# A recurrent attention and expert-gate kernel: the second output tile moves to bank_b, the experts' second product becomes two rounded passes

## What is computed

```python
xn = _layernorm(x, axis=-1)
# attention
q = (xn @ wq.T); k = (xn @ wk.T); v = (xn @ wv.T)        # 32, 8, 8 heads of 128
q = q * cos + _rotate_half(q) * sin; k = k * cos + _rotate_half(k) * sin
scores = einsum('bhqd,bhkd->bhqk', q, repeat(k)) / sqrt(128)  # scaled by key range, causal
attn = einsum('bhqk,bhkd->bhqd', softmax(scores), repeat(v))
s = attn.reshape(b, 256, 4096) @ wo.T
# experts
gates = softmax(top2(xn @ router_w.T))
mid = einsum('tf,erf->ter', xn, A)
all_deltas = einsum('ter,eor->teo', mid, B) * 4.0
g = silu(einsum('te,teo->to', gates, all_deltas))
return x + s * g
```

## Time and profile before

| | |
|---|---|
| median of 3 runs | 1377.58 us (1376.59 to 1377.71) |
| the profiled execution | 1377.09 us |
| its span, first to last instruction | 1375.3 us |
| mean granted TensorE clock | 0.991 |
| busy: PE, PE weight loads, DVE, ACT, POOL | 1335.1, 1105.3, 964.8, 962.2, 423.8 us |

### The profile page before, as it was taken

The page is one execution under the profiler, slowest core; times in us unless marked ns, Lnnn a source line. Parts: engine busy times, 40 slices in busy tenths (PEclk is TensorE's granted clock), DMA queues, the critical chain, the costliest instruction groups (busy, mean ns, idle before and its releaser), DMA issues.

```text
span 1375.3 us, 22613 instructions
## 1 busy us (share of the span) xinstructions
PE 1335.1 (97%) x6982; PEld 1105.3 (80%) x6982; DVE 964.8 (70%) x2444; ACT 962.2 (70%) x2512; POOL 423.8 (31%) x341
## 2 busy tenths in 40 slices
PE   7699999999999999999999999999999999999997
PEld 5588787777788888888888888888888888888885
DVE  6776577666766676776767677666777767668775
ACT  3687567667777767787777777777777767776773
POOL 5332221413414133143322234141331433224321
PEclk9799999999999999999999999999999999999998
DMA  5000000201101000000000001000000100012223
GB/s 210 16 16 14 23 16 9 69 24 31 69 1 31 0 23 23 0 31 15 23 8 15 15 15 31 0 31 0 23 23 0 31 15 23 8 43 87 69 81 104
DMA packets 23302, 43.48 MB, mean 32 GB/s; under 512 B 2464, under 2 KB 2592, under 8 KB 23264
## 3 DMA queue, kind: packets, MB, share of 16 engines
q1 hardware_dynamic: 20592, 37.76, 8.8%
q10 hardware_dynamic: 2672, 5.25, 1.0%
HBM read 34.61 MB, written 8.39 MB: 31 GB/s over the span
## 4 chain that ended last, share of the span: by engine, by line
PE 91%; DVE 5%; ACT 1%; issue 1%; DMA 1%; POOL 0%; DVEq 0%; SPq 0%; ACTq 0%
PE o_ps L542 26%; PE bank_a L447 18%; PE bank_b L447 18%; PE pv_ps L533 10%; PE pair L517 7%; PE pair L524 5%; PE pair L513 2%; DVE y_sum L1119 1%; PE o_ps L493 1%; PE pair L515 1%; PE bank_a L503 1%; PE o_ps L447 1%; DMA x_sb<-x 1%; DVE x_sb L946 0%; DVE xT_lo L959 0%
## 5 line engine op out<-in xcount | busy, mean ns | idle before, releaser
L362 POOL TENSOR_TENSOR rot<-rot,tab 128x512 f32<-128x512 f32 x160 | 208.6, 1306 | 611.5 <-ACT rot L749 611.3
L792 ACT ACTIVATE probs<-probs,row_min 128x128 f32<-128x128 f32 (+1 forms) x512 | 225.6, 447 | 0.0
L811 ACT ACTIVATE pT_hi<-pair 128x768 fp32r<-128x768 f32 x128 | 103.9, 812 | 170.2 <-PE pair L524 169.4
L542 PE MATMUL o_ps<-w_hi,attn_hi 128*128 128x512 f32 x504 | 206.8, 410 | 8.1 <-DVE y_sum L1119 7.0
L803 ACT ACTIVATE probs<-probs,row_inv 128x128 f32<-128x128 f32 (+1 forms) x512 | 190.8, 446 | 26.6 <-DVE row_inv L1109 26.3
L542 PE MATMUL o_ps<-w_hi,attn_lo 128*128 128x512 f32 x504 | 198.4, 394 | 0.0
L542 PE MATMUL o_ps<-w_lo,attn_hi 128*128 128x512 f32 x504 | 197.0, 391 | 0.0
L1079 DVE TENSOR_TENSOR pT_lo<-pair,pT_hi 128x768 fp32r<-128x768 f32 x128 | 121.5, 949 | 91.8 <-ACT pT_hi L811 91.6
L347 POOL TENSOR_TENSOR w_hi<-raw,zero 128x512 fp32r<-128x512 f32 x74 | 84.7, 1144 | 256.4 <-PE bank_a L447 135.6
L447 PE MATMUL bank_b<-xT_hi,w_hi 128*128 (+1 forms) x380 | 153.0, 403 | 2.4 <-DVE xT_lo L959 2.4
L447 PE MATMUL bank_a<-xT_hi,w_hi 128*128 (+1 forms) x380 | 154.6, 407 | 0.4 <-DVE xT_lo L959 0.4
(11 more groups left out here) (160 smaller groups left out, 2984.7 us busy)
## 6 DMA issues: line engine op xcount, KB each, us to landing
raw<-w_seq SPq DMA_DIRECT2D x76, 256.0 KB, 2.6
gate_scratch<-silu ACTq DMA_DIRECT2D x16, 256.0 KB, 2.0
out<-y_sum SPq DMA_DIRECT2D x16, 256.0 KB, 2.0
x_sb<-x SPq DMA_DIRECT2D x3, 1024.0 KB, 12.0
silu<-x SPq DMA_DIRECT2D x8, 256.0 KB, 2.7
silu<-gate_scratch SPq DMA_DIRECT2D x8, 256.0 KB, 2.8
bT_full<-x SPq DMA_DIRECT2D x7, 256.0 KB, 2.8
gmT_full<-gate_scratch SPq DMA_DIRECT2D x7, 256.0 KB, 3.0
```

Source lines behind the costliest of these rows:

```text
L362: nc.gpsimd.tensor_tensor(v, v, tab[:, s:s + SEQ].unsqueeze(1).to_broadcast([P, 2, SEQ]), ALU.mult).then_inc(sin_done[kind], 1)
L542: mm = nc.tensor.matmul(bank[:, :], a[:, h, rows], w[:, WO + h, :], start=(h == 0 and i == 0), stop=(h == GROUP - 1 and i == 2))
L792: a = nc.scalar.activation(s, s, ACT.Exp, bias=row_min[:, j % 2, i:i + 1], scale=-1.0, accum_out=row_sum[:, i:i + 1])
L811: nc.scalar.activation(pT_hi[:, :, :], pair[j % 2][:, :, 0:ROWS], ACT.Copy).then_inc(pThi_done, 1)
```

## The change

The second output tile of each pair, (0,1) and (1,1), is written to bank_b instead of o_ps, and DVE adds it from there. Tile (1,0) now waits for the addition of tile (0,0) (count 4u - 3) instead of tile (0,1); tile (1,1) and tile (0,1) wait that bank_b is free of H0 (in unit 30 of H3); the projection of H2 waits for the addition of tile (1,1). Side steps wait for one addition fewer. Tile (0,0) waits once for the last chunk of output weights. The last two tiles of all use pair0 instead of bank_a and bank_b.

The experts' second product becomes two fp32r passes: gm_T holds the rounded gate tile in partitions 0 to 63 and its remainder in 64 to 127, b_hi holds the rounded weights twice, b_lo the remainder once. The first pass has 128 contraction rows (both halves of gm_T with b_hi), the second 64 (rounded gate tile with b_lo). ACT rounds b in unit 1, DVE subtracts in unit 2; a gt step has ACT round and DVE subtract. The d steps go to slots 0 and 2 only, WRITTEN becomes 8, and the last d stands in slot (7,2,0). One buffer (b_raw) takes all gate tiles on their way out; it is stored in the slot behind its d. The sets xg take other buffers: mid, raw (loaded once the last weight chunks are split) and parts of rot and cosx (loaded behind the store of tile 11).

```diff
-WRITTEN = 7
+WRITTEN = 8
-        bT, gm_T = bT_full[0:ER, :], gmT_full[0:ER, :]
-        silu = sb("silu", [P, 2, DM])
+        b_raw = sb("b_raw", [P, DM])
+        b_hi = sb("b_hi", [P, DM], F32R)
+        b_lo_full = sb("b_lo", [P, DM], F32R)
+        b_lo = b_lo_full[0:ER, :]
+        gm_T = sb("gm_T", [P, BLOCK], F32R)
+        silu = b_raw
-        xg = [(silu[:, 0, :], silu[:, 1, :]), (bT_full[:, :], gmT_full[:, :]), (raw[:, 0, :], raw[:, 1, :])]
+        xg = [(mid_flat[:, 0:DM], mid_flat[:, DM:2 * DM]), (raw[:, 0, :], raw[:, 1, :]), (rot[:, 0, :], cosx[:, 0, :])]
-        places += [at for at in free if at >= (1, 2, 1) and at[2] != 3][:len(steps) - len(places)]
+        later = [at for at in free if at >= (1, 2, 1)]
+        for what, _ in steps[len(places):]:
+            while later[0][2] not in ((0, 2) if what == "d" else (0, 1, 2)):
+                later.pop(0)
+            places.append(later.pop(0))
...
-            load_xg(1, 1)
             for c in range(CHUNKS - 2, CHUNKS):
                 sp.wait_ge(w_ready[c], KV_HEADS)
-            load_xg(TILES - 1, 2)
+            load_xg(1, 1)
...
+            sp.wait_ge(q_ready[H2], UNITS)
+            load_xg(TILES - 1, 2)
             store_tile(TILES - 4)
...
-            tiles = 4 * u
+            tiles = max(0, 4 * u - 1)
...
-                nc.tensor.matmul(o_ps[:, :], gm_T[:, t * P:(t + 1) * P], bT, start=True, stop=True)\
+                nc.tensor.matmul(o_ps[:, :], gm_T[:, t * P:(t + 1) * P], b_hi[:, :], start=True, stop=False)
+                nc.tensor.matmul(o_ps[:, :], gm_T[0:ER, t * P:(t + 1) * P], b_lo, start=False, stop=True)\
                     .then_inc(side_ps, 1)
...
-            output_heads(b, t, o_ps, range(GROUP), weights=weights).then_inc(o_done, 1)
+            if weights is not None:
+                pe.wait_ge(w_ready[CHUNKS - 1], weights)
+            output_heads(b, t, (o_ps, bank_b)[t][:, :], range(GROUP)).then_inc(o_done, 1)
...
-                output_tile(1, 0, n4[0], n4[-2], uses=uses(0))
+                output_tile(1, 0, n4[0], n4[-3], uses=uses(0))
...
-                output_tile(1, 1, n4[0], n4[-1])
+                if not last:
+                    bank_free(H0, c2)
+                output_tile(1, 1, n4[0], n4[-2])
...
-                bank_free(H0, c2)
+                if first:
+                    bank_free(H0, c2)
+                else:
+                    pe.wait_ge(y_added, n4[0])
                 project(H2, bank_b, WQ + 2, x_1, w_1)
...
-            output_tile(0, 0, n4[2], None if first else n4[0], weights=w_0, uses=uses(3))
+            output_tile(0, 0, n4[2], None if first else n4[-1], weights=w_0, uses=uses(3))
...
-            output_tile(0, 1, n4[2], n4[1])
+            if not last:
+                bank_free(*((H0, c3) if ahead else (H3, c2)))
+            output_tile(0, 1, n4[2], n4[0] if last else None)
...
-                output_heads(1, t, (bank_a, bank_b)[t], range(0, 2))
+                output_heads(1, t, pair[0][:, t, :], range(0, 2))
...
-                nc.scalar.activation(gm_T, o_ps[0:ER, :], ACT.Copy).then_inc(side_out, 1)
+                nc.scalar.activation(gm_T[0:ER, :], o_ps[0:ER, :], ACT.Copy).then_inc(gmhi_done, 1)
...
+        def b_high():
+            nc.scalar.wait_ge(b_in, 32)
+            nc.scalar.activation(b_hi[:, :], b_raw[:, :], ACT.Copy).then_inc(bhi_done, 1)
...
-            nc.scalar.dma_start(bT, b_t).then_inc(bT_in, 16)
+            for half in range(2):
+                nc.scalar.dma_start(b_raw[ER * half:ER * (half + 1), :], b_t).then_inc(b_in, 16)
...
+        def split_b():
+            nc.vector.wait_ge(bhi_done, 1)
+            nc.vector.tensor_tensor(b_lo, b_raw[0:ER, :], b_hi[0:ER, :].bitcast(F32), ALU.subtract)\
+                .then_inc(blo_done, 1)
...
+            elif what == "gt":
+                dve.wait_ge(gmhi_done, i + 1)
+                nc.vector.tensor_tensor(gm_T[ER:, :], o_ps[0:ER, :], gm_T[0:ER, :].bitcast(F32), ALU.subtract)\
+                    .then_inc(side_out, 1)
```

More of the change, by code:

```diff
@@ L156, in build @@
         ar_in = sem("ar_in")
-        bT_in = sem("bT_in")
+        b_in = sem("b_in")
+        bhi_done = sem("bhi_done")
+        blo_done = sem("blo_done")
+        gmhi_done = sem("gmhi_done")
         stat_done = sem("stat_done")
@@ L263, in slots @@
         def slots(eng, u):
-            return {c: value(eng, 4 * u + c) for c in range(-2, 8)}
+            return {c: value(eng, 4 * u + c) for c in range(-3, 8)}
         def units(eng, u):
@@ L534, in prob_value, with output_heads @@
             mm.then_inc(pv_done, 1)
-        def output_heads(b, t, bank, heads, weights=None):
+        def output_heads(b, t, bank, heads):
             rows = slice(SEQ * b + P * t, SEQ * b + P * (t + 1))
             for h in heads:
-                if weights is not None:
-                    nc.tensor.wait_ge(w_ready[WO + h], weights)
                 for i, (a, w) in enumerate(((attn_hi, w_hi), (attn_hi, w_lo), (attn_lo, w_hi))):
-                    mm = nc.tensor.matmul(bank[:, :], a[:, h, rows], w[:, WO + h, :], start=(h == 0 and i == 0),
+                    mm = nc.tensor.matmul(bank, a[:, h, rows], w[:, WO + h, :], start=(h == 0 and i == 0),
                                           stop=(h == GROUP - 1 and i == 2))
@@ L699, in _ @@
             for t in range(2):
-                output_heads(1, t, (bank_a, bank_b)[t], range(0, 2))
+                output_heads(1, t, pair[0][:, t, :], range(0, 2))
             pe.wait_ge(attn_ready, n)
             for t in range(2):
-                output_heads(1, t, (bank_a, bank_b)[t], range(2, GROUP)).then_inc(o_done, 1)
+                output_heads(1, t, pair[0][:, t, :], range(2, GROUP)).then_inc(o_done, 1)
         def x_high(t, bank):
@@ L1109, in row_inverse, with add_tile @@
             nc.vector.reciprocal(row_inv[:, :], row_sum[:, :]).then_inc(inv_done, 1)
-        def add_tile(tile, done, start=False, final=None, bank=o_ps, xg_set=None, tail=False):
+        def add_tile(tile, done, start=False, final=None, bank=None, xg_set=None, tail=False):
             dve = nc.vector
@@ L1139, in tile_in @@
                 add_tile(value(nc.vector, (4 * u + k - back + TILES) % TILES), value(nc.vector, 4 * u + k + 1 - back),
-                         start=isinstance(u, int) and u - b < BLOCKS, final=final, xg_set=t)
+                         start=isinstance(u, int) and u - b < BLOCKS, final=final, bank=(o_ps, bank_b)[t][:, :], xg_set=t)
             rows_low(0, n4[1])
@@ L1260, in _ @@
                 t = TILES - 2 + i
-                add_tile(t, n - 1 + i, final=t, bank=(bank_a, bank_b)[i], xg_set=2 * i, tail=True)
+                add_tile(t, n - 1 + i, final=t, bank=pair[0][:, i, :], xg_set=2 * i, tail=True)
 def kernel(**inputs):
```

31 lines of the change are left out of this document (16 added, 15 removed).

## The result

| | before | after |
|---|---|---|
| time, median of the runs on the same chip | 1377.09 us (1375.54 to 1377.71) | 1357.77 us (1356.87 to 1358.82) |
| ratio after / before, with its 95% interval | | 0.9862 [0.9845, 0.9879] |
| profiled execution, its span | 1377.09, 1375.3 us | 1357.92, 1356.1 us |
| mean granted TensorE clock | 0.991 | 0.990 |

A forecast was written before the change was run, and what follows sets the result against it. TensorE's own sequence and its gaps were taken to bound the kernel (91% of the span). 15.3 + 11.4 - 0.3 = 26.4 us, so 1377.58 - 26.4 = 1351.2 us; 8 in 10 range 1348.0 to 1357.0.

The forecast's parts named there:

- Part 1: Unit boundaries, second output tile to bank_b: tile (1,0) no longer waits for tile (0,1)'s addition, 15.3 us saved.
- The cover: New bank_b waits and tile (0,0)'s wait for output weights: other PE work covers them, so they cost nothing.
- The 0.6 lost in the closing units: Units 28 to 31: gate multiplication before pT_lo makes PE wait about 0.3 at each of two boundaries, -0.6 us.
- Part 2: Experts' second product as two fp32r passes, 0.46 for both: 12.6 us saved less 1.2 of waits, 11.4 us.
- (b): Experts' second product: 64-row pass costs 0.63 instead of 0.23, or switching rows costs a bubble; 6.4 us, 1357.6 us, chance 0.08.
- The waits beside it: Side steps in units 4 to 7: K projection waits for v_T, d for the gate's low half; 1.2 us.
- The one gate buffer: Gate tiles' transfer out: d comes at least two slots later, the transfer lands 2.0 us after issue; nothing to 0.1.
- Start: Kernel start: ACT issues the 128 KB of expert weights twice; 0.3 us lost, at most 0.9.
- (a): Unit boundaries: the next scores wait for pT_lo, 0.25 lost at 21 looped boundaries; 5.2 us, 1356.4 us, chance 0.08.
- (d): Tile (0,1) in 31 units: H0's cosine product is late; at 2.0 us later the time is 1384 us, chance 0.02.
- (e): Tile (1,0)'s wait count still includes tile (0,1), so the bank change gains nil; 1366.5 us, chance 0.03.
- (c): Side steps hide more than reckoned and the start costs nothing: 28.5 us, 1349.1 us; chance 0.07 with the skill's gap.

The follow-up runs named there:

- delay experiments: Kernel after with one idle DVE addition ahead of pT_lo in each of the 20 looped units, 256 or 512 columns wide: 1369.28 and 1374.20 us.
- the last experiment: Kernel after with 128-row second pass, expert-weight loads in unit 1, and units 28 to 30 multiplying tile (0,1) by its gate behind pT_lo: 1349.50 us.
- the 128-row pass: Kernel after with the second pass of each d step on 128 contraction rows instead of 64: 1351.44 us.

## Why the prediction was wrong, point by point

**What bounds.** Right: what moved the time were PE's sequence and its gaps.

**Part 1, 15.3 us.** Right in mechanism and size: 15.9 alone by the medians, 15.0 by the steps. The boundary gave 0.54 a unit by start to start, although the list of waits called only 0.29 of it idle. The delay experiments show the same from the other side: a wait of the scores costs its lateness and a restart of 0.11 us. At the output tile no such restart shows, as its second product follows at 0.34 with the wait (737.41 to 737.75) and at 0.32 without it. The cover held at all the places named: no wait of an output tile for H0's cosine, for the first addition or for the last chunk of weights stands in PE's list. The 0.6 lost in the closing units were seen, and won back in the last experiment.

**Part 2, 11.4 us: the failed step.** "A pass with 64 contraction rows isn't in this trace" was right, and both bounds were worked out: 0.46 and 0.86 a step. I took the lower, by a row whose passes all have 128 contraction rows and differ in their output rows. Measured are 0.85. The nearest row was the other one: its product has 64 contraction rows, and the bubble around it, 0.32 us in and 0.34 behind, is the one found now, though its data type differs. Choosing by type and not by row count cost 16 x 0.39 = 6.2 us of the sum, and rival (b), 1357.6 us, got 0.08 where it should have been near even. The stated range ended at 1357.0, and so left out (b)'s own 1357.6, although the text says that it takes in most of it. The sign given for (b), the two products 0.4 or more apart, was wrong as well: they are 0.32 apart in the row above, and most of the loss lies behind the pass. The waits beside it were about right: 0.4 was forecast for unit 7, and with the 128-row pass 0.33 shows as idle (start to start 0.73, where the earlier trace rows has 0.39); units 4 to 6 lose about 0.3 each in its profile, 0.25 were forecast. The one gate buffer and the splits on ACT and DVE show no wait of PE. The 0.23 us between products stood in every row after, nowhere the 131 ns that the Trainium skill gives (TensorE: Matmul & The Clock Gate, Back-to-back issue gap).

**Start, -0.3 us.** Too small: 1.2 to 1.7 at a like clock, 1.1 to 2.8 by the medians. The bound above, 0.9, was the time of the transfer alone. I had said "nothing if they come behind the x tiles"; they do not, and the 0.6 us of later landing then pull the normalisation into POOL's work. Which of the two sets the loss stays open, since taking the stretch away gave nothing.

**Sum.** 26.4 + 0.6 (part 1) - 6.2 (the pass) - 0.9 to 1.4 (the start beyond its 0.3) = 19.4 to 19.9 us; measured 19.3.

**Rivals.** (b) came true in place and size, 6.2 us against its 6.4. That its 1357.6 us lies only 0.2 from the measured time is in part luck, since the 0.6 more of part 1 and the 0.9 to 1.4 of the start nearly cancel. (a) did not: 0.23 to spare was enough, and 0.05 would have been. (d) and (e) have no trace. (c) was out with (b).

## What to carry to other kernels

In a dense stream of products like this one, keep the contraction rows of neighbours alike: pad a short pass to 128 rows with data that does no harm rather than save rows. Where a cost has two bounds, take the row that shares the unusual property of the new operation, and give the other bound's case real weight. A wait of an engine that issues ahead costs more than its recorded idle time, so take it from start to start, and price a small instruction on the releasing engine by its distance to the next start, not by its size.

## What the runs showed of the hardware

- A pass with 64 contraction rows between passes with 128 costs 0.62 us instead of 0.23 (fp32r, 512 columns); a second one directly behind it 0.24. The Trainium skill (TensorE: Matmul & The Clock Gate, Why this matters for your kernels) says of a product with 32 contraction rows that it takes as long as one with 128. Carried over to 64 rows, the pass would have cost 0.23, an estimate. The measurement decides: here that holds between neighbours of equal row count, not across the change.
- Restart after a wait: the first product of the scores starts 0.05 to 0.06 us after the end of what releases it, and the second 0.11 later than in a running stream.
- Four SBUF-only tensor-scalar operations of 128x512 fp32 on DVE take 1.91 us with POOL idle and 5.74 us beside POOL's two-input operations (2.94 to 5.80 over the other profiles, where POOL works beside them for a part or all of the time).
- An addition of 64x256 on DVE with nothing to wait for, recorded as 0.42 us, put the start of its successor 0.55 us later behind the reciprocal, one of 64x512 (0.69 recorded) 0.82. Counted from the transposes, pT_lo ends at 3.18, 3.86 and 4.14 us.
- The time of an execution moves with its mean granted TensorE clock: 1374.9 to 1376.3 us at 0.994 or 0.995, 1378.8 to 1379.1 at 0.988 or 0.989, for the same kernel.
